# Sixteen-head causal attention: a large tile's turns dealt to two steps, values one step later

## The reference, cut to what matters

```python
def _L2_attn_ref(x, W_K, W_Q, W_V, W_O):          # x is (2, 1024, 128) here
    k = jnp.einsum('ihd,bpd->biph', W_K, x)
    q = jnp.einsum('ihd,bpd->biph', W_Q, x)
    v = jnp.einsum('ihd,bpd->biph', W_V, x)
    scores = jnp.einsum('biph,biqh->biqp', k, q)
    masked = scores * mask - NEG * (1.0 - mask)
    attn = jax.nn.softmax(masked / np.sqrt(D_HEAD), axis=-1)
    z = jnp.einsum('biph,biqp->biqh', v, attn)
    ...
    out = jnp.einsum('df,bqf->bqd', W_O, z_flat)
x = x + _layernorm(_L2_attn_ref(_layernorm(x), W_K, W_Q, W_V, W_O))
```

## Time and profile before

| | |
|---|---|
| runs of the kernel before | 3275.61 us median of 3 (3275.44 to 3277.61) |
| profiled execution | 3277.67 us, its span 3275.8 us |
| the stage of 16 heads, first scores to last output matmul | 1216.7 to about 1858 us |
| TensorE matmuls, whole span | 2875.9 us busy, 88% |
| VectorE / ScalarE / GpSimd, whole span | 2098.4 (64%) / 1586.7 (48%) / 1007.0 us (31%) |

### The profile page before, as it was taken

One profiled execution on the slowest core, in us unless ns is written; L12 is line 12 of the kernel. 1 busy time (PEld: TensorE's weight loads), 2 busy tenths in 40 slices (PEclk: granted clock), 3 DMA queues, 4 the chain that ended last, 5 costly groups with the idle time before them and its releaser, 6 DMA issues. The chain is left out here.

```text
span 3275.8 us, 56202 instructions
## 1 busy us (share of the span) xinstructions
PE 2875.9 (88%) x21938; PEld 1781.0 (54%) x21958; DVE 2098.4 (64%) x4384; ACT 1586.7 (48%) x3087; POOL 1007.0 (31%) x710
## 2 busy tenths in 40 slices
PE   8985999998899989999999788979877889877698
PEld 4552555566666656666666655646653334334465
DVE  5568999735533355664655566556655999997545
ACT  4334888733322234444544465545636767643122
POOL 3211000000000014443444354234515768773000
PEclk9985999989899999999999989989999999999799
DMA  1000000001000010000000000000002444431000
GB/s 52 1 3 1 3 3 3 3 2 78 26 1 1 1 54 1 1 1 1 1 1 1 23 5 1 1 1 1 1 16 99 144 144 143 143 140 40 1 1 13
DMA packets 22584, 94.72 MB, mean 29 GB/s; under 512 B 2288, under 2 KB 4464, under 8 KB 21552
## 3 DMA queue, kind: packets, MB, share of 16 engines
q1 hardware_dynamic: 22320, 91.12, 7.9%
HBM read 89.80 MB, written 1.31 MB: 28 GB/s over the span
## 5 line engine op out<-in xcount | busy, mean ns | idle before, releaser
L1747 POOL TENSOR_TENSOR many_probs<-many_probs,many_rinv 128x2048 f32<-128x2048 f32 (+7 forms) x128 | 269.8, 2108 | 361.5 <-DVE many_rinv L1783 361.5
L1002 DVE TENSOR_REDUCE heads_halfmax<-heads_qmajor 128x1 f32<-128x512 f32 x512 | 316.4, 682 | 32.3 <-PE heads_qmajor L863 28.9
L3129 DVE TENSOR_TENSOR_SCAN stream_state<-stream_decay,stream_state 128x512 f32<-128x512 f32 x256 | 306.3, 1233 | 0.5
L967 ACT ACTIVATE weights<-heads_kmajor 128x1024 f32<-128x1024 f32 x256 | 259.4, 1027 | 71.7 <-PE heads_kmajor L875 65.6
L1720 ACT ACTIVATE many_probs<-many_score,many_negmax 128x1024 f32<-128x1024 f32 (+7 forms) x256 | 187.6, 738 | 173.6 <-DVE many_negmax L1767 173.6
L221 POOL TENSOR_TENSOR norm_rstd<-norm_rstd,neghalf 128x4 f32<-128x4 f32 x60 | 61.1, 1019 | 659.0 <-DVE norm_rstd L178 659.0
L1767 DVE TENSOR_REDUCE many_negmax<-many_score 128x1 f32<-128x1024 f32 (+7 forms) x256 | 184.5, 752 | 111.6 <-PE many_score L1649 109.9
L2799 PE MATMUL stream_yacc<-stream_state,ident 128*128 128x512 f32 x512 | 249.1, 614 | 0.4 <-POOL stream_state L3091 0.4
L1459 PE MATMUL swiglu_gate_up<-HT,weights 128*128 128x512 f32 x512 | 244.8, 602 | 0.0
L2961 ACT ACTIVATE stream_decay<-weights,mamba_negA 128x512 f32<-128x512 f32 x256 | 173.0, 689 | 112.1 <-DVE stream_state L3129 110.8
L3091 POOL TENSOR_TENSOR stream_state<-XN,stream_state 128x1024 f32<-128x1024 f32 x85 | 200.4, 2361 | 79.9 <-DVE stream_state L3129 79.4
(11 more groups left out here) (494 smaller groups left out, 6113.2 us busy)
## 6 DMA issues: line engine op xcount, KB each, us to landing
XN<-mamba_crows SPq DMA_DIRECT2D x85, 512.0 KB, 3.6
stream_crow<-mamba_crows SPq DMA_DIRECT2D x43, 512.0 KB, 3.7
weights<-in_w_dram SPq DMA_DIRECT2D x1, 6148.0 KB, 17.1
weights<-in_w_dram SPq DMA_DIRECT2D x1, 4274.0 KB, 13.9
weights<-in_w_dram SPq DMA_DIRECT2D x1, 3296.0 KB, 10.8
weights<-in_w_dram SPq DMA_DIRECT2D x1, 2112.0 KB, 7.9
weights<-in_w_dram SPq DMA_DIRECT2D x1, 2102.0 KB, 8.2
weights<-in_w_dram SPq DMA_DIRECT2D x1, 2048.0 KB, 8.5
```

Of the source, the lines that this page charges most:

```text
L967: nc.scalar.activation(probs_of(k).rearrange("p (a n) -> p a n", a=2), kmajor[:, at:at + 2, :], ACT.Exp, scale=SC).then_inc(exp_done, 1)
L1002: nc.vector.tensor_reduce(halfmax[:, g % 2, at, h % 2:h % 2 + 1], qmajor[:, (2 * n + j) % 3, :], AX, ALU.max).then_inc(max_done, 1)
L1747: nc.gpsimd.tensor_tensor(pair, pair, rinv[:, n % 4, :].unsqueeze(2).broadcast_to([P, 2, wide]), ALU.mult).then_inc(norm_done, 1)
L3129: nc.vector.tensor_tensor_scan(h[:, part(half)], decay[:, (2 * g + half) % DECAYS, :], h[:, part(half)], 0.0 if half == 0 else h[:, BANK - ...
```

## The change

The plan of a step, with n the unit scored:
- The scores are issued in two parts. Part 0 is, for a large tile, the first 512 columns of both heads; part 1 is the rest and the mask. For a small tile part 0 is empty.
- Turns 0 and 1 stay at unit n - 3. Turns 2 and 3 are those of unit n - 4: turn 2 between the two parts, turn 3 behind part 1. Units with a third turn are large, and so they meet the scores of a large tile.
- Values are those of unit n - 5, so that a large tile's step has the values of a small one, and the other way round.
- The output projection of a finished batch moves from the fourth to the sixth step of the group after it.
- `probs` becomes three large buffers, the third being `m.XN`, a tile of the layer norm that is free then, and two small ones (`small`); `probsT` has 3 buffers, `rowsum` and `rinv` 5.

```diff
             for k in range(min(f, 2)):
                 fill("turn", (n - 3, k), ("act", "dve")[k % 2])
             if n < N:
-                step.append(("scores", n, None, None, None))
-            for k in range(2, f):
-                fill("turn", (n - 3, k), ("act", "dve")[k % 2])
-            if 4 <= n < N + 4:
-                fill("values", n - 4, "dve")
+                step.append(("scores", (n, 0), None, None, None))
+            late = fills(n - 4) if 4 <= n < N + 4 else 0
+            if late > 2:
+                fill("turn", (n - 4, 2), "act")
+            if n < N:
+                step.append(("scores", (n, 1), None, None, None))
+            if late > 3:
+                fill("turn", (n - 4, 3), "dve")
+            if g >= 1 and at == 5 and g % PAIRS == 0:
+                for half in range(2):
+                    fill("out", (g // PAIRS - 1, half), "act")
+            if 5 <= n < N + 5:
+                fill("values", n - 5, "dve")
             if g + 1 < len(GROUPS) and at in (0, 1, 2, 3, 5, 6):
                 fill("project", (g + 1, (0, 1, 2, 3, None, 4, 5)[at]), "dve")
-            if g >= 1 and at == 3 and g % PAIRS == 0:
-                for half in range(2):
-                    fill("out", (g // PAIRS - 1, half), "act")
...
-                if n >= 2:
+                if part == 0 and n >= 2:
                     pe.wait_ge(exp_done, 2 * (n - 1))
-                wide = (i + 1) * P
-                for at in range(0, wide, BANK):
+                if part == 0 and wide <= BANK:
+                    return
+                for at in [x for x in range(0, wide, BANK) if wide <= BANK or x // BANK == part]:
...
-                for h in range(2):
+                for h in range(2 * part):
                     nc.tensor.matmul(score_of(n, h)[:, i * P:wide], m.identb[:], m.causalb[:], start=False, stop=True,
                                      skip_group_check=True).then_inc(s_done, 1)
...
+        def probs_of(n):
+
+            if n % 2:
+                return small[:, n // 2 % 2, :]
+            return probs[:, n // 2 % 3, :] if n // 2 % 3 < 2 else m.XN[:].rearrange("p t n -> p (t n)")
...
-                if n >= 4:
-                    act.wait_ge(rinv_done, n - 3)
-                    act.wait_ge(fill_done, turn_fill[n - 4, fills(n - 4) - 1] + 1)
+                if n >= 5:
+                    act.wait_ge(rinv_done, n - 4)
+                old = n - (6, 4)[n % 2]
+                if old >= 0:
+                    act.wait_ge(fill_done, turn_fill[old, fills(old) - 1] + 1)
```

More of the change, by code:

```diff
@@ L1586, in causal_sixteen_heads @@
         v = ph.sb("v", [P, 2, TPB, P])
-        probs = ph.sb("probs", [P, 4, 2 * SEQ])
-        probsT = ph.sb("probsT", [P, 2, 2 * SEQ])
+        probs = ph.sb("probs", [P, 2, 2 * SEQ])
+        small = ph.sb("small", [P, 2, SEQ])
+        probsT = ph.sb("probsT", [P, 3, 2 * SEQ])
         negmax = ph.sb("negmax", [P, 3, 2])
-        rowsum = ph.sb("rowsum", [P, 4, 2])
-        rinv = ph.sb("rinv", [P, 4, 2])
+        rowsum = ph.sb("rowsum", [P, 5, 2])
+        rinv = ph.sb("rinv", [P, 5, 2])
         zT = ph.sb("zT", [P, PAIRS, SEQ])
@@ L1631, in project, with scores @@
                     last.then_inc(fill_done, 1)
-            def scores(n):
+            def scores(n, part):
                 g, i = UNITS[n]
-                if n % 8 == 0:
-                    for part in range(4):
-                        engine, at = project_at[g, part]
+                wide = (i + 1) * P
+                if part == 0 and n % 8 == 0:
+                    for piece in range(4):
+                        engine, at = project_at[g, piece]
                         pe.wait_ge(kept[engine], at)
-                if n >= 2:
+                if part == 0 and n >= 2:
                     pe.wait_ge(exp_done, 2 * (n - 1))
-                wide = (i + 1) * P
-                for at in range(0, wide, BANK):
+                if part == 0 and wide <= BANK:
+                    return
+                for at in [x for x in range(0, wide, BANK) if wide <= BANK or x // BANK == part]:
                     to = min(wide, at + BANK)
@@ L1657, in turn @@
                     last = nc.tensor.transpose(ring[:, k % 2, x % 4 * P:(x % 4 + 1) * P],
-                                               probs[:, n % 4, x * P:(x + 1) * P], m.ident[:])
+                                               probs_of(n)[:, x * P:(x + 1) * P], m.ident[:])
                 last.then_inc(fill_done, 1)
@@ L1674, in values @@
                                                 v[:, g % 2, kb, DH * h:DH * (h + 1)],
-                                                probsT[:, n % 2, x * P:(x + 1) * P], start=(kb == 0), stop=(kb == i),
+                                                probsT[:, n % 3, x * P:(x + 1) * P], start=(kb == 0), stop=(kb == i),
                                                 skip_group_check=True)
@@ L1689, in _ @@
                 if what == "scores":
-                    scores(idx)
+                    scores(*idx)
                     continue
@@ L1703, in turned_part @@
             at, to = 4 * f * P, min(4 * f + 4, 2 * (UNITS[n][1] + 1)) * P
-            return probsT[:, n % 2, at:to], ring[:, k % 2, 0:to - at]
+            return probsT[:, n % 3, at:to], ring[:, k % 2, 0:to - at]
         @block.scalar
@@ L1745, in _ @@
                 pool.wait_ge(rinv_done, n + 1)
-                pair = probs[:, n % 4, 0:2 * wide].rearrange("p (h w) -> p h w", h=2)
-                nc.gpsimd.tensor_tensor(pair, pair, rinv[:, n % 4, :].unsqueeze(2).broadcast_to([P, 2, wide]),
+                pair = probs_of(n)[:, 0:2 * wide].rearrange("p (h w) -> p h w", h=2)
+                nc.gpsimd.tensor_tensor(pair, pair, rinv[:, n % 5, :].unsqueeze(2).broadcast_to([P, 2, wide]),
                                         ALU.mult).then_inc(norm_done, 1)
@@ L1780, in invert @@
                 dve.wait_ge(exp_done, 2 * (n + 1))
-                if n >= 4:
-                    dve.wait_ge(norm_done, n - 3)
-                nc.vector.reciprocal(rinv[:, n % 4, :], rowsum[:, n % 4, :]).then_inc(rinv_done, 1)
+                if n >= 5:
+                    dve.wait_ge(norm_done, n - 4)
+                nc.vector.reciprocal(rinv[:, n % 5, :], rowsum[:, n % 5, :]).then_inc(rinv_done, 1)
             for n, step in enumerate(STEPS):
```

4 lines of the change are left out of this document (2 added, 2 removed).

## The result

The changed kernel takes 3319.62 us (median of four runs, 3318.58 to 3322.37) against 3275.53 us before (four runs, 3275.27 to 3277.61): slower by 1.35%, a ratio of 1.0135, 95% interval 1.0117 to 1.0152. The forecast was 3314, with a range of 3290 to 3329. The profiled execution has a span of 3316.7 us, 40.9 more than before.

A forecast was written before the change was run, and what follows sets the result against it. TensorE was taken to bound the 16-head stage. Waits +1.83, restarts 0.25 and split 0.42 made +2.5 us a group; fourteen full groups plus the first and last gave +39, so 3314 us, range 3290 to 3329.

The forecast's parts named there:

- fourteen full groups: Groups of eight steps in the 16-head stage, each forecast to lose 2.5 us, together 35 us.
- The chain behind the scores: After large scores TensorE waits for VectorE's maxima and zT copy: 1.09, 0.62, 1.39, 0.94 us (tiles 7, 6, 5, 4).
- ScalarE's waits go: Small values no longer wait for ScalarE's copy of the third turn; 1.0 us a group goes.
- Rival C: Much slower: ScalarE's first turn copy holds the values in tiles 7 and 5, +0.9 a group more, 3328 us; chance 0.10.
- Second turns behind the projection's copy: Second turns wait for the projection's copy, 1.33 us a group instead of 1.71; turns restarting after waits add 0.25.
- The split: Large tiles' scores issued in two halves cost 0.10 to 0.12 us, four times: +0.42 a group, ends 0 and 0.8.
- Sum: Per group in the 16-head stage: waits +1.83, restarts +0.25, split +0.42, together +2.5 us.
- TensorE's busy time stays within 1%: Predicted sign over the profile: TensorE's busy time changes by no more than 1%.
- Buffers and output projection: Extra buffers cost nothing; moving the output projection two steps, done twice, costs nothing or at most 1 us.
- Rival A: Faster: turns after large scores don't meet zT's copy, only removed waits count, -19 us, 3257 us; chance 0.07.
- Rival B: Same: split free, steps 5 and 4 hide the turn copy, waits cancel, 3276 to 3282 us; chance 0.05.
- Rival D: TensorE's clock falls to 1.2 GHz in some stretch of each batch, 3340 us or more; chance 0.02.

The follow-up runs named there:

- half_maxima: The changed kernel with the maximum of a large tile taken over only the first half of its columns: 3288.7 us, ratio 1.0040.
- before_half_maxima: The kernel before the change with the maximum of a large tile taken over only the first half of its columns: 3273.4 us, ratio 0.9991.
- values_later: The changed kernel with turns 2 and 3 back at unit n - 3 behind the scores, only the values staying one step later: 3308.8 us, ratio 1.0101.
- split_alone: swap_and_invert with the last of the first turns put between the halves of a large tile's scores: 3278.5 us, ratio 1.0008.
- buffers_only: The schedule of the kernel before with only the changed kernel's buffers and place of the output projection: 3275.6 us, ratio 0.9999.
- whole_scores: The changed kernel with turns 2 and 3 behind undivided scores and the fourth turn's copy between the two maxima: 3276.5 us, ratio 1.0000.
- swap_and_invert: The kernel before with the projection ahead of the values in steps 0 and 4, and VectorE's reciprocal ahead of the copies in small steps: 3255.5 us, ratio 0.9937.

## Why the prediction was right, point by point

The direction, the mechanism and the size were right: a group was to lose 2.5 and lost 2.86, the whole +39 and it was +40.9 on the profiled execution. (By the medians it is +38 and +44.1: of the changed kernel the fastest of the four runs was profiled, of the one before the slowest.) From the first to the last normalisation of tile 7 it is 586.75 us before and 628.98 after, +42.2; the rest of the program differs by -1.3. The working had counted fourteen full groups; there are twelve (+2.86 each), the change of batch (+3.3), the first (+1.8, forecast 1) and the last (+2.8, forecast 3.2). The sum has two parts, though, and they were off in opposite ways.

- *The chain behind the scores.* Forecast 2.66 us after tile 7 with a wait of 1.09; measured 2.66 and 1.10. After tile 6 0.62, measured 0.62. In step 5 1.39, measured 1.31. In step 4 0.25 and 0.69, measured 0.22 and 0.66. half_maxima against before_half_maxima shows the cause and not only the place.
- *ScalarE's waits go.* Forecast 1.0 a group to nothing; the matmuls' wait went from 12.4 to 1.4 us. Rival C, that ScalarE's first turn copy would hold the large values, did not come about.
- *Second turns behind the projection's copy.* This term was too high: 1.33 + 0.25 a group forecast, about 1.1 measured. After a first turn that has waited, eight turns take 1.18 us (1417.70 to 1418.88), where in the kernel before they took 1.30 (1408.00 to 1409.30): VectorE starts the projection's copy 0.20 after zT's (1417.57 and 1417.37), before it was 0.30 (1407.96 and 1407.66). The same in three steps is a good part of why values_later came out under its expectation.
- *The split.* This is the term that was mis-sized: +0.42 forecast, about +1.4 measured. In the changed kernel all waits of a group, counted as in the prediction, are 1.10 + 0.62 + 1.31 + 0.88 + 1.1 = 5.0, and 41.32 less that leaves 36.3 of bare work, against 34.9 before: +1.4. split_alone gives 1.38 by another way, and the busy time a third (19.7 us in the changed kernel, 23.0 in split_alone, by 16 groups 1.2 and 1.4). Two things were wrong in the working. First, I set 1.06 + 1.19 for two tiles of 512 columns against 2.14 for one of 1024, which gives +0.11, but the 1.19 ends at a turn behind the mask and the 2.14 at values behind it. The trace of before has both masks:

```profile
1400.98 0.29 PE L1649 MATMUL many_score<-causalb,identb 128*128 128x128 bf16 x2
...
1405.12 0.29 PE L1649 MATMUL many_score<-causalb,identb 128*128 128x128 bf16 x2
```

From the mask to the turn it is 0.13 (1401.11) and to the values 0.22 (1405.34). The scores without the mask are 1.06 twice against 1.92 (1403.20 to 1405.12), so +0.20, the figure that split_alone has. It could have been read before the change. Second, I charged the turn nothing for standing alone, though I had put that at 0.06 to 0.1 in the bounds. In the changed kernel the four transposes between the halves take 0.59 (1413.18 to 1413.77) in place of 0.43, +0.16; in step 7 the two parts make 0.36, and the upper end of 0.8 for four was too low as well. The page of the Trainium skill that I set against my charge (TensorE: Matmul & The Clock Gate, Step-by-step: a weight load is pulled ahead of running matmuls if nothing conflicts) pointed to a still smaller one. As I applied it, split_alone would have taken 3255 us, and it took 3278: the measurement decides. The page makes the pull-ahead depend on loads that don't conflict; the trace shows no load pulled ahead at either change between a transpose over the full array and scores on half of its rows, so the page's condition may not have been met there. No run tests that.
- *Sum.* Waits +1.45 where 2.1 were forecast (restarts included), bare work +1.4 where 0.42 was. The two errors, -0.6 and +1.0, cancel in part (+0.36 is left), and that the total is close is in this part luck.
- *The prediction said that TensorE's busy time stays within 1%.* It rose by 0.7%; true by the letter, and the 19.7 us in it were just what was missed. Of a change of 1.3% a bound of 1% on the largest engine says too little. The working for 40 us of the stage (37.9 x 38.46 / 41, plus the split) gives 36.0 and not the 36.4 that it states; measured were 36.54.
- *Buffers and output projection.* Nothing in the whole time, as said (buffers_only). In its trace the change of batch, where the output projection has moved, takes 1.0 us longer (53.34 in place of 52.36 between two normalisations of tile 7), the upper end of what was allowed for.
- *Rival A* (faster) would have needed a cover as long as the chain; whole_scores gives the cover back and comes to the time of before, not below it, since its values wait for ScalarE again in steps 5 and 4 (0.25 and 0.47 us, where in the kernel before it was steps 1 and 2). *Rival B* (same) would have needed a free split and a hidden turn copy, and both cost. *Rival D*: the clock stayed at 1.00.

What stays open: what keeps the loads back. The rows place the 0.33 (0.20 in the scores that start twice, 0.13 in the turn by itself) but don't say whether it is the sequencer, the change between half and full rows, or the loads. It isn't peculiar to scores and turns: in swap_and_invert the values behind a turn (1356.69) and the projection behind values (1361.87) start together with their own loads too, and there the number of columns changes, while the turn behind a mask, both on all rows and columns, has its load at 1356.10 and starts at 1356.16. That fits a change in the part of the array that is used, but no experiment varied it alone.

## What to carry to other kernels

When two engines take turns on a small ring of buffers, count for each long operation of the engine that frees the slots what the other one has to do meanwhile: moving work ahead of the semaphore that starts the long operation takes that cover away, though the amount of work is the same. Look at the waits of the baseline one by one before a schedule is rebuilt: two swaps of neighbours, each priced from the timeline, gave 0.6% where the larger redesign lost 1.3%. And charge the places where a stream of matmuls is interrupted by another kind, as the scores are here by a turn; it doesn't show as idle time of the matmuls, only as a longer busy time for the same count.

## What the runs showed that I had not expected

- At a change between scores on 64 rows and transposes on 128, the weight load starts with its own matmul, while within the scores it runs ahead (1359.24 in swap_and_invert). One such insertion costs 0.33 us in step 7, and 62 of them 23 us.
- All of that is hidden in the busy time: 2870 to 2877 us without it, 2893 to 2896 with it, for the same matmuls (21938 or 21958 records in kernels of either kind).
- The full groups within a batch repeat to within some 0.01 us (one in each of the last two kernels is 0.1 longer), so that a period read from two neighbouring groups tells differences of 0.05 us which the whole run's time (0.2% is 6.5 us) can't: 38.46 and 38.40 for before and whole_scores.
